# A macaron block on one core: two second-layer groups in plain float32 with one silu pass each, and the layer norm's normalisation on GpSimd

## The reference

```python
x = x + 0.5 * ffn(layernorm(x))
x = x + attn(layernorm(x))
x = x + 0.5 * ffn(layernorm(x))

def ffn(x):                      # layer norm once more, inside
    h = layernorm(x) * gamma + beta
    y = silu(h @ w1 + b1)        # w1: 256 x 1024, integers times scales
    return x + 0.5 * (y @ w2 + b2)   # w2: 1024 x 256, one scale for every 128 rows and column
...
# attn: a = sigmoid(x Wa + ba), b = x Wb + bb, c = tanh(x Wc + bc);
# s_t = a_t s_(t-1) + (1 - a_t) b_t ; out = (c s) Wy + by + x Wd + bd
```

## Time and profile before

| what | value |
|---|---|
| median of 3 runs | 860.97 us |
| lowest and highest run | 858.55 and 861.0 us |
| span of the profiled execution, from first to last instruction | 856.8 us |
| TensorE busy | 811.6 us, 95% |
| VectorE busy | 808.8 us, 94% |
| ScalarE busy | 658.6 us, 77% |
| GpSimd busy | 558.6 us, 65% |

### The profile page before, as it was taken

One profiled execution on the slowest core, in us unless ns is written; L12 is line 12 of the kernel. 1 busy time (PEld: TensorE's weight loads), 2 busy tenths in 40 slices (PEclk: granted clock), 3 DMA queues, 4 the chain that ended last, 5 costly groups with the idle time before them and its releaser, 6 DMA issues.

```text
span 856.8 us, 15154 instructions
## 1 busy us (share of the span) xinstructions
PE 811.6 (95%) x3682; PEld 624.0 (73%) x3682; DVE 808.8 (94%) x1645; ACT 658.6 (77%) x1083; POOL 558.6 (65%) x430
## 2 busy tenths in 40 slices
PE   1699999999999999999999998999999999999997
PEld 0477777777777778766777766777777777777785
DVE  4899999999999999979999997999999999999975
ACT  3488888888888888745655657888888888888884
POOL 4566777777667767735655656766677676776763
PEclk9999999999999999999999999999999999999999
DMA  8710000000000000000000000000000011000001
GB/s 258 236 48 2 2 0 0 0 0 0 0 0 0 0 0 1 2 1 1 0 0 0 0 1 1 0 26 25 24 24 24 24 35 38 25 24 24 26 25 50
DMA packets 20619, 20.33 MB, mean 24 GB/s; under 512 B 1590, under 2 KB 20332, under 8 KB 20588
## 3 DMA queue, kind: packets, MB, share of 16 engines
q1 hardware_dynamic: 19180, 17.86, 6.6%
q10 hardware_dynamic: 1312, 2.10, 0.7%
q0 software_dynamic: 96, 0.00, 0.0%
HBM read 11.57 MB, written 8.39 MB: 23 GB/s over the span
## 4 chain that ended last, share of the span: by engine, by line
PE 81%; DVE 11%; issue 4%; ACT 2%; DMA 1%; POOL 1%; DVEq 0%; ACTq 0%; POOLq 0%
PE ps_z L802 40%; PE ps_fc L802 26%; PE ps_fc L892 5%; PE ps_tr L795 3%; PE ps_tr L844 3%; DVE xhat L564 3%; DVE y_sb L587 2%; DVE z_acc L609 1%; PE ps_fc L900 1%; PE ps_fc L886 1%; DVE stats L537 1%; DMA resid<-in_L_attn_x 1%; DVE resid L578 1%; DVE resid L706 1%; PE ps_z L795 1%
## 5 line engine op out<-in xcount | busy, mean ns | idle before, releaser
L349 POOL TENSOR_TENSOR g_lo<-g_full,g_hi 128x512 fp32r<-128x512 f32 x256 | 334.9, 1308 | 187.5 <-ACT g_hi L463 181.1
L447 ACT ACTIVATE u_sb<-ps_fc,cols 128x512 f32<-128x512 f32 x256 | 199.0, 777 | 68.3 <-PE ps_fc L802 65.3
L802 PE MATMUL ps_fc<-h_hi,q_sb 128*128 128x512 f32 x512 | 218.2, 426 | 14.1 <-DVE y_sb L587 6.4
L802 PE MATMUL ps_fc<-h_lo,q_sb 128*128 128x512 f32 x512 | 204.0, 398 | 0.0
L609 DVE SCALAR_TENSOR_TENSOR z_acc<-ps_z,cols,z_acc 128x512 f32<-128x512 f32 x256 | 189.3, 741 | 11.1 <-PE ps_z L802 10.7
L587 DVE SCALAR_TENSOR_TENSOR y_sb<-ps_fc,cols,u_sb 128x512 f32<-128x512 f32 x256 | 189.3, 740 | 10.0 <-ACT u_sb L447 10.0
L461 ACT ACTIVATE g_full<-y_sb 128x512 f32<-128x512 f32 x256 | 159.7, 624 | 37.6 <-DVE y_sb L587 37.6
L564 DVE TENSOR_SCALAR xhat<-resid,mean_var,rstd 128x256 f32 (+1 forms) x192 | 167.3, 917 | 3.3 <-POOL rstd L335 3.3
L463 ACT ACTIVATE g_hi<-y_sb 128x512 fp32r<-128x512 f32 x256 | 158.5, 619 | 0.0
L802 PEld LDWEIGHTS ps_fc<-h_hi,q_sb 128*128 128x128 f32 x512 | 97.2, 190 | 49.0 <-DVE y_sb L587 24.3
L802 PE MATMUL ps_z<-g_hi,q_sb 128*128 128x512 f32 x288 | 116.8, 405 | 3.0 <-DVE z_acc L607 2.6
(11 more groups left out here) (97 smaller groups left out, 1164.4 us busy)
## 6 DMA issues: line engine op xcount, KB each, us to landing
resid<-in_L_attn_x SPq DMA_DIRECT2D x16, 512.0 KB, 4.2
out_x<-resid SPq DMA_DIRECT2D x16, 512.0 KB, 2.9
q_int<-in_L_ffn_fc_q ACTq DMA_DIRECT2D x2, 1024.0 KB, 8.8
z_acc<-in_L_ffn_fc_scales SPq DMA_DIRECT2D x1, 256.0 KB, 8.0
wd_sb<-in_L_attn_Wd SPq DMA_DIRECT2D x1, 256.0 KB
z_acc<-in_L_ffn_fc_scales SPq DMA_DIRECT2D x1, 192.0 KB, 8.6
resid<-in_L_attn_Wy SPq DMA_DIRECT2D x2, 64.0 KB
wab_sb<-in_L_attn_Wa SPq DMA_DIRECT2D x1, 64.0 KB
```

The source lines that it names most:

```text
L349: nc.gpsimd.tensor_tensor(g_lo[:, slot % 4, :], g_full[:, slot % 2, :], g_hi[:, slot % 4, :].bitcast(F32), ALU.subtract).then_inc(g_ready, 1)
L447: nc.scalar.activation(u_sb[:, f % 2, :], ps_fc1[:, f % 2, 0, :], ACT.Identity, bias=col(R_B1 + f), scale=col(R_S1 + f)).then_inc(u_ready, 1)
L802: last = nc.tensor.matmul(out, w, v, start=start and i == 0, stop=stop and i == len(pairs) - 1)
```

## The change

Groups 0 and 1 of the second product (`NATIVE = 2`) become plain float32. ScalarE runs their silu once (`g_native`), GpSimd subtracts nothing for them, and TensorE multiplies in float32 with weights that hold their scales (`w2_full`); both halves of both groups sum up in PSUM, and ScalarE fetches the two sums. The other six groups (`SPLIT`) are all unscaled: two matmuls and one addition on VectorE for each half. The seven scaled and split half groups are gone.

The four normalisation blocks of a tile move from VectorE to GpSimd (`normalise`), and with them the terms of the variance; a third small instruction makes the negative mean, because the GpSimd version adds it. The steps of the layer norm's work move: statistics from steps 1, 2 to 4, 5; the power from 2 to 6; normalisation from 4, 5 to 6, 7; the residual's scaling from 6 and the following 0 to 4 and 5 of the next tile. GpSimd's program is written out for all tiles (`each_tile`) instead of looping.

```diff
-    SCALED = (4, 3)
+    NATIVE = 2
+    SPLIT = FC - NATIVE
+    SUMS = SPLIT + 1
...
+    RESIDUAL_AT = (4, 5)
+    STATISTICS_AT = (4, 5)
+    VARIANCE_AT = 5
+    RSQRT_AT = 6
+    NORMALISE_AT = (6, 7)
+    TURN_AT = (1, 3)
...
+            def rsqrt(ln, twice):
+                pool.wait_ge(aggr_done, ln + 1)
+                wait(pool, xhat_ready, ln)
+                nc.gpsimd.tensor_scalar(var_terms[:, 0:SUB], mean_var[:, :, 1], EPS, 1.0, ALU.add, ALU.mult)
+                if twice:
+                    nc.gpsimd.tensor_scalar(var_terms[:, SUB:2 * SUB], mean_var[:, :, 1], 1.0 + EPS,
+                                            EPS * EPS, ALU.mult, ALU.add)
+                nc.gpsimd.tensor_scalar(neg_mean[:, :], mean_var[:, :, 0], -1.0, 0.0, ALU.mult,
+                                        ALU.add).then_inc(terms_ready, 1)
+                pool.wait_ge(terms_ready, ln + 1)
...
+            def normalise(ln, t, twice, blocks=range(SUB)):
+                if blocks[0] == 0:
+                    pool.wait_ge(rstd_ready, ln + 1)
+                    wait(pool, turned, 2 * ln)
+                at = SUB if twice else 0
+                for a in blocks:
+                    last = nc.gpsimd.tensor_scalar(xhat[:, a, :], resid[:, t, a, :], neg_mean[:, a:a + 1],
+                                                   rstd[:, at + a:at + a + 1], ALU.add, ALU.mult)
...
+                if native(g):
+                    wait(act, fc2_done, 2 * step - 14)
+                    nc.scalar.activation(g_native[:, g, :], y_sb[:, g % 4, :], ACT.Silu).then_inc(g_hi_ready, 1)
+                    return
...
+                    if native(g):
+                        last = nc.tensor.matmul(bank_of(g, n, par), w2_full[:, g, at], g_native[:, g, :],
+                                                start=g == 0, stop=g == NATIVE - 1)
+                    else:
+                        last = products(bank_of(g, n, par), [(w[:, g - NATIVE, at], v[:, split_slot(g, par), :])
+                                                             for w in q2_parts for v in (g_hi, g_lo)])
...
-            def normalise(ln, t, twice, blocks=range(SUB)):
-                    last = nc.vector.tensor_scalar(xhat[:, a, :], resid[:, t, a, :], mean_var[:, a, 0:1],
-                                                   rstd[:, at + a:at + a + 1], ALU.subtract, ALU.mult)
```

More of the change, by code:

```diff
@@ L268, in over_tiles, with each_tile @@
             tile(NT - 1, 1, 2, 0)
+        def each_tile(tile):
+            for t in range(NT):
+                tile(t, t % 2, min(t, 2), min(NT - 1 - t, 2))
         block = ctx.enter_context(nc.Block())
@@ L373, in tile @@
                     for f in range(FC):
[L374 to L379, removed]
-                        if f == RSQRT_AT and (behind >= 2 or ff0 == 0):
-                            rsqrt(ln + 2, 2 * SUB if behind >= 2 else SUB)
+                        if f >= 1:
+                            g_low(ff, f - 1, par)
+                        elif before:
+                            g_low(ff - 1, FC - 1, 1 - par)
@@ L638, in tile @@
                                 add_mixer(NT - 1, 1, half)
-                        if behind >= 1 and f == 0:
-                            residual(ff + 1, t + 1, range(2, SUB))
+                        if behind >= 1 and f in RESIDUAL_AT:
+                            residual(ln + 1, ff + 1, t + 1, halves[RESIDUAL_AT.index(f)])
                         if ff0 == 0 and not before and f == 3:
@@ L651, in tile @@
                             if f == VARIANCE_AT:
-                                variance(ln + 2, twice)
-                            if f in NORMALISE_AT[not before]:
-                                normalise(ln + 2, t2, twice, halves[NORMALISE_AT[not before].index(f)])
-                            if f == RESIDUAL_AT[not before] and twice:
-                                residual(ff + 2, t + 2, range(2))
+                                variance(ln + 2)
                         if before and f in ADD_AT:
@@ L757, in mixer_tile @@
                     statistics(t2)
[L758 removed]
+                    variance(t + (NT + 2))
                 scan(t, par)
@@ L761, in mixer_tile @@
                 nc.vector.tensor_tensor(c_sum, ps_c[0:N, :], c_part, ALU.add).then_inc(c_sum_ready, 1)
-                def norm():
-                    normalise(t + (NT + 2), t2, twice)
-                    if twice:
-                        residual(NT + t2, t2, range(2 if t2 else SUB))
-                if behind:
-                    norm()
                 if before:
@@ L775, in mixer_tile @@
                 nc.vector.tensor_tensor(cs_full, c_sb[:, par, :], state[:, par, :], ALU.mult).then_inc(cs_ready, 1)
-                if not behind:
-                    norm()
+                if behind == 1:
+                    residual(t + (NT + 2), NT, 0)
             over_tiles(dve, mixer_tile)
```

293 lines of the change are left out of this document (131 added, 162 removed).

## The result

The changed kernel takes 871.86 us (870.55 to 873.32, 4 runs) against 860.99 us (858.55 to 861.78, 4 runs) before in the same session: a ratio of 1.0133, 95% interval 1.0114 to 1.0152. It is 1.3% slower. The profiled execution has a span of 868.7 us, 11.9 more than before's 856.8, at a mean granted clock of TensorE of 0.994 (before 0.998; 1 is full speed).

The account below looks back on a forecast made before the run. VectorE was taken to bound at 20.58 us a tile; after the change GpSimd's loop at 20.6. 29 x (20.6 - 20.58) = +0.6, edges -8: span 849.4, plus 4.2: 853.6, said 853. Range 829 to 884, forecast's own 845 to 860.

Parts of the forecast that it names:

- I take 0: Mixer: TensorE busy throughout, GpSimd gains 13.1 us on 24.3 but stays under 40, so no change in time.
- b: Time of one normalisation block of 256 columns on GpSimd, taken as 0.45 us, between 0.29 and 0.80.
- at nearly nothing: Extra VectorE time from `resid` blocks meeting GpSimd's subtractions in steps 4 and 5; possible range 0 to 3.2 us.
- What bounds the kernel before: Feed-forward stages: VectorE bounds at 20.58 us a tile, TensorE 0.6 us behind; 29 such distances, 597 of 857 us.
- TensorE's part: 22 float32r matmuls go, 5.1 us; four float32 ones come, 0.86 us each, 3.4 us; TensorE then needs 18.3 us.
- The loop over GpSimd: From step 1's transposes to the next tile's, through GpSimd's subtraction, power and blocks: 20.6 us a tile.
- 3a + 4b: Three small instructions and four blocks on GpSimd, added to 18.2 us of the loop: 0.6 + 1.8 us.
- a: Time of one small layer norm instruction on GpSimd, taken as 0.20 us, between 0.10 and 0.29.
- GpSimd slower: Rival 4: b of 0.55 gives 21.0 us a tile and 865; b of 0.80, a of 0.29 give 902; chance 0.18.
- rival 3: `resid` blocks wait for subtractions; VectorE's work becomes 21.0 us a tile, 865 us; mean block about 1.0 us; chance 0.14.
- Rivals 3 and 4: The two slower cases: VectorE held up in its `resid` blocks, chance 0.14; GpSimd's blocks slower than taken, chance 0.18.
- The edges: Start of the program 4 us less, end 4 us less, first feed-forward stage's tail about even; together -8 us.

Follow-up runs that it names:

- Experiment 4: Kernel before with the two native float32 groups alone, normalisation and variance terms staying on VectorE, residual scaling at steps 0 and 1: 880.56 us, ratio 1.0239.
- the first two experiments: Changed kernel with one edit each: residual scaling moved to steps 1 and 2, 882.53 us; transposes of `xhat` one step later, 866.09 us.
- experiment 3: Changed kernel with residual scaling at steps 1 and 2 and the transposes of `xhat` one step later: 865.36 us, ratio 1.0067.
- Experiment 5: Changed kernel with the turn into the last stage reordered: GpSimd takes `cs` low part first, VectorE's residual scaling and statistics go behind the scan: 867.56 us.
- Experiments 7 to 10: Changed kernel, layer norm work earlier: 829.55 us; blocks back at steps 6, 7: 833.2; instead GpSimd reordered: 819.45; that plus reordered turn into last stage: 816.42.
- the best version: Changed kernel with earlier layer norm work, GpSimd's low parts of `h` and power reordered, and the turn into the last stage reordered: 816.42 us, ratio 0.9473.
- experiments 6 and 7: Changed kernel, residual at steps 1, 2; statistics 1, 2, power 2, blocks 4, 6: 871.91 us; or statistics 2, 3, power 3, blocks 5, 6: 829.55 us.
- experiments 1 and 8: Changed kernel with residual scaling at steps 1, 2: 882.53 us; the same with statistics at 2, 3, variance and power at 3, blocks at 6, 7: 833.2 us.
- experiment 11: Kernel before with normalisation and variance terms on GpSimd, without native groups, residual scaling at step 7 and step 0 of the next tile: 961.94 us, ratio 1.1168.
- experiment 7: Changed kernel with residual scaling at steps 1, 2, statistics at 2, 3, variance and power at 3, blocks at 5, 6: 829.55 us, ratio 0.9648.

## Why the prediction was wrong

The forecast was 7.4 us less of span, measured are 11.9 more: 19.3 apart. In the measured split 9.5 of these come from the mixer and the turns at its ends, for which I had written "I take 0", 6.8 from the steady tiles (b, and the `resid` blocks that I took "at nearly nothing"), 3.0 from the edges. The measured tile of 20.87 us, put into my own sum, gives 29 x 0.29 - 8 = +0.4: no change. What makes the kernel slower, and not merely equal, is what the mixer and its turns cost.

**What bounds the kernel before: right.** Experiment 4 puts two additions on VectorE, and 1.1 of their 1.3 us show in the tile. But 25 distances are steady, not 29 (13 and 12): the first two of each stage are of another length (24.85 and 23.32 us, 19.10 and 23.10).

**TensorE's part: right.** Float32 products follow each other at 0.86 us (at 223.84 four passes, that is two products, in 1.88 us with the end of the last), and the engine is idle 3.8 us of 40 where it was full.

**The loop over GpSimd: right in kind, 20.6 against 20.87.** To the subtraction's start it takes 13.40 us (197.38 to 210.78) for my 13.47. From there to the transposes 7.47 (210.78 to 218.25): three small instructions 0.27 apart, not 0.20; a block 0.53, not 0.45; the waits for its own results 0 and 0.11, not 0.25 each. The sum 3a + 4b was 2.4 and is 2.95, with b the larger part (+0.35) and a +0.2; the two waits, the other way, took back 0.4. The misjudged term is b. I had worked out that nothing is won from b = 0.51 on, and took the value below it because the select looked nearer in kind; its weight in the text was a chance of 0.18 for "GpSimd slower". The select reads two scalars less, and no row supported doubling it rather than more.

**"I take it at nearly nothing": wrong.** The `resid` blocks did meet subtractions: +0.85 and +1.5 us a pair and +0.4 for the scale, 2.8 us, which ate the whole cover of 2.8 us that I had counted and no more. It was rival 3, whose condition (a mean block near 1.0 us) was nearly met: 0.93 over all blocks, 0.96 in this tile. My count of places was a count along an undisturbed loop; TensorE's steps have other lengths once it waits, and a gap of GpSimd worked out to a few tenths of a microsecond is no gap to rely on. Rivals 3 and 4 both came, 0.14 us apart. As their limits don't add up (the later one counts), each alone explained the tile. That is why the first two experiments recovered nothing or 0.14 us; behind both stood the third limit of experiment 3, at 20.66.

**The mixer "I take 0": wrong by 2.4, and the turn behind it, which I had not costed, by 6.8 (with 0.3 on the way in, 9.5).** My sum for GpSimd there, 37.4 of 40, was near the measured 38.4; from so full an engine I should have asked who waits in its queue. Experiment 5 gives the price of two such positions. The mixer's own 2.4 us no experiment isolates; that a wait in GpSimd's queue is behind them is argued.

**The edges**: the start gave 3.2 of 4, the end 1.8 of 4. In sum, in the measured split: steady distances +7.4 where my sum had +0.6, mixer and the turns at its ends +9.5 instead of 0, edges -5.0 instead of -8: +11.9 of span.

**What the forecast did not ask**: whether the order itself was the loss. The sums (TensorE 18.3, VectorE 17.8) promised some 70 us, and 45 were there (0.9473 of 861). Experiments 7 to 10 get them with the same instructions. What holds the best version at 19.3 instead of 18.3 us is only argued: VectorE's crowded steps 1 to 3, where the bank for the float32 product comes free late.

## What to carry to other kernels

When work moves to an engine with spare time, its sum is the smaller question: write down its queue with times, and ask for each instruction who waits behind it, both for its result and merely in line. An instruction that needs a late result (the power, a scale) stands best just behind work that is ready anyway; a schedule with it one step earlier cost 42 us here (experiments 6 and 7, where statistics and blocks moved too), one with it three steps later 49 (experiments 1 and 8, statistics and variance with it, some of it clock). When one limit is found, look for a second within a few tenths of a microsecond before believing that removing the first will pay.

## What the runs showed of the hardware that I had not expected

- GpSimd's `tensor_scalar` with two scalars per partition takes 0.53 us start to start for 128x256 float32 and 0.27 for 128x4; the latter took 1.17 us beside VectorE's scan in the mixer (`var_terms`, 516.81; the scan at 516.72, 1.28 us).
- The hold between VectorE and GpSimd is uneven: VectorE's `tensor_scalar` of 256 columns out of SBUF went from 0.41 to a median of 0.94 us, while the mean of GpSimd's subtractions is 1286 ns in the changed kernel, where they meet, and 1298 in experiment 7, where they don't. The Trainium skill (SBUF — State Buffer, Who interferes with whom) has the later one wait for the other's whole instruction. The 2.50 us for 128x4 elements in experiment 11 are longer than any one of the instructions that GpSimd ran beside it, three subtractions in a row:

```profile
242.06 3.91 POOL L374 TENSOR_TENSOR g_lo<-g_full,g_hi 128x512 fp32r<-128x512 f32 x3
```

- A TensorE that stands 2.5 us in each tile lost clock in some tiles (granted 0.91 over a stretch of 20 us) and took 1.5 us more in each of these; with 1.7 us of standing in each, the changed kernel kept 1.00 in its steady tiles. At its turn into the last stage, after 3.60 us of standing, the granted clock fell to 0.56 over 10 us.
